# Projections of the next head group one unit earlier, and that group's weight split moved between two output scalings

## The chip, the core and the metric

The kernel runs on one core of one Trainium2 chip. The metric is the device time of one execution in microseconds (us); less is better. The engines are TensorE (PE in the profile; its weight loads are PEld), VectorE (DVE), ScalarE (ACT), GpSimd (POOL) and SyncE (SP), which here only issues DMAs. Each engine works through its own instructions in order and waits on semaphores for the others. SBUF is the on-chip memory, PSUM the banks that TensorE writes.

## What is computed

One hybrid transformer layer over x of 4 batches, 1024 tokens and 512 features, float32. The part that matters here is its first block, causal attention with 16 heads of 32:

```python
kqv = x @ Wqkv + bqkv                      # x: 4 x 1024 x 512
q, k, v = parts of 512 features each       # 16 heads of 32
scores = einsum('bsnh,btnh->bnst', k, q) / sqrt(32)    # upper triangle kept
attn = softmax(scores, axis=2)
out = einsum('bnkq,bnkh->bqnh', attn, v) @ Wo + bo
```

After it come an expert feed-forward block, a state-space block and the feed-forward block once more. The change touches none of them.

## The kernel before

A loop runs over the 4 batches. In the attention part of a batch the 16 heads form 4 groups of 4 (a group is 128 of the 512 features), and a group forms 2 pairs of 2 heads: the first pair has `hf` 0 and the second `hf` 1, so a batch has 8 pairs, p0 to p7, and a new group begins at each even one.

The work of a pair is cut into 12 units, u0 to u11, each a block of 128 keys by up to 512 queries. TensorE issues, in this order by hand: in unit u the scores of unit u+1 (`scores_b`, L859), then the weighing of the values by unit u's exponentials (`weigh`, L876 and L878), then, in u2 to u7, score tiles of the next pair of which only the row maxima are wanted (`scores_a`, L839; 16 tiles, `AHEAD` says which in which unit; a tile waits for a certain number of earlier maxima, as it takes their banks). In u9 the 16 maxima are transposed for the next pair. In the last unit the scores are already those of the next pair's u0.

In the first pair of a group that is not the last, TensorE also makes the next group's projections: four chunks (`project`, L724 to L726), each 12 matmuls of 512 columns into PSUM bank 7, one behind each unit named in `PROJECT_AT`. A chunk's result is read by ScalarE (`project_hi`, L1214, the rounded part, behind the exponential of the unit after) and then by VectorE (`project_lo`, L1541, the remainder); both write `EV`. When the fourth chunk's remainder is there, SyncE copies `EV` by 12 DMAs into the stacks `QS` and `KS` of the next group's first pair (L463), six for each head. `scores_a` in u2 of the second pair reads the first six.

VectorE takes the row maxima (L1565). The outputs and the softmax sums of 512 queries (a half, c 0 or c 1) lie in PSUM bank 6. `take` (L1571) copies them to `OS`, in u3 for half 0 and behind u11 for half 1. `invert` (L1578) makes `rec`, the reciprocals: in two parts in u8 and u9 for half 0, and in one part behind the second `take` for half 1. GpSimd then multiplies `OS` by `rec` (L1870, the output scaling, `o_scaled`). A `take` waits until GpSimd has scaled the half before it, because it writes over `OS`; and the first weighing into bank 6 for a new half (u0 for half 0, u4 for half 1) waits for that `take`. VectorE's order in a pair is this:

```python
for u in range(UNITS):
    if u == 3:
        take(p, 0)
    if not (last and hf):
        for t16 in AHEAD.get(u, ()):
            maximum(p + 1, t16)
    if hf == 0 and not last and u in PROJECT_AT:
        project_lo(g + 1, PROJECT_AT.index(u), False)
    if u in (8, 9):
        invert(p, hf, 0, u - 8, 2)
take(p, 1)
invert(p, hf, 1, 0, 1)
```

The weights of a group arrive by two DMAs in `win_raw`. ScalarE rounds them (`group_hi`, L1184, in u1 of the first pair, `qkw_hi`), GpSimd subtracts the rounded part (`group_lo`, L1808, `qkw_lo`), and the first projection chunk waits for that. Semaphore waits are written `signal.wait(engine, n, k)`, which means that k events of round n have happened. GpSimd also copies a group's values to `VG` (L1833).

Of the kernel before, what the change touches and what calls it, by code (L numbers as in the profile page):

```python
# [29 lines left out]
GROUPS = HEADS * HS // P  # L30
# [9 lines left out]

AHEAD = {2: (0, 1, 2, 3), 3: (4, 5), 4: (6, 7), 5: (8, 9, 10, 11), 6: (12, 13), 7: (14, 15)}
TURN_AT = 9
PROJECT_AT = (4, 6, 8, 10)

MAX_BANK = [0, 1, 2, 3, 0, 2, 0, 2]
MAX_FREE = [-1, -1, 0, 0, 2, 4, 5, 6]
# [90 lines left out]
def hybrid_layer(nc, x, Wqkv, bqkv, Wo, bo, W_in, conv_w, conv_b, z_bias, Dskip, W_out,  # L137
                 Wr, br, Wd, bd, Wu, bu, out):
    with ExitStack() as ctx:
# [6 lines left out]
        def signal(name, per):  # L146
            return Signal(sem(name), per)
# [101 lines left out]
        qkw_lo = signal("qkw_lo", 1)  # L249
# [441 lines left out]
        def _(pe):  # L691
# [100 lines left out]
            with pe.Fori(0, NB) as b:  # L792
# [20 lines left out]
                def project(g, ch, first=False):  # L813

                    w, c = ch // 2, ch % 2
                    if ch == 0:
                        qkw_lo.wait(pe, b * 4 + g, 1)
                    elif not first:
                        pj_lo.wait(pe, b * 4 + g, ch)
                    cols = slice(c * HB, (c + 1) * HB)  # L820
                    for k in range(KT):
                        i = three(ps[:, 4 + ch if first else 7, :], win[:, 0, w, 0, k, :], win[:, 0, w, 1, k, :],
                                  uh[:, k, cols], ul[:, k, cols], k == 0, k == KT - 1)
                    i.then_inc(pj.sem, 1)

                def scores_a(p, slot, occ, t16):

                    hh, t = t16 // TT, t16 % TT
                    if t == 0:
                        pe.wait_ge(s_stack[slot][hh], occ * 96 + 96)  # L830
                    free = MAX_FREE[t] + hh * TT
                    if free > 0:
                        a_max.wait(pe, p, free)
                    b0 = MAX_BANK[t]
                    n = (t + 1) * P
                    for c in range(0, n, HB):
                        m = min(HB, n - c)
                        diag = c + m == n
                        i = pe.matmul(ps[:, b0 + c // HB, 0:m], QS[slot][0:STACK, hh, t * P:(t + 1) * P],  # L839
                                      KS[slot][0:STACK, hh, c:c + m], start=True, stop=not diag)  # L840
                        if diag:
                            i = pe.matmul(ps[:, b0 + c // HB, m - P:m], identb[:, :], mask_ts[:, :], start=False, stop=True)  # L842
                    i.then_inc(a_pe.sem, 1)
# [71 lines left out]
                for last in (False, True):  # L915
                    with (pe.Fori(0, GROUPS - 1) if not last else ExitStack()) as i_:
                        g = GROUPS - 1 if last else i_
                        for hf in range(2):
# [3 lines left out]
                            for u in range(UNITS):  # L922
# [9 lines left out]
                                if ahead:  # L932
                                    for t16 in AHEAD.get(u, ()):
                                        if t16 == 2:
                                            ex.wait(pe, p, 3)
                                        scores_a(p + 1, 1 - hf, occ + hf, t16)
                                if hf == 0 and not last and u in PROJECT_AT:
                                    project(g + 1, PROJECT_AT.index(u))

# [193 lines left out]
        def _(act):  # L1133
# [27 lines left out]
            def experts(n, f, meanwhile=None):  # L1161
                def exponentials(h):
                    hs = slice(h * HALF, (h + 1) * HALF)
                    g_in.wait(act, f, h + 1)
                    act.activation(gex[:, hs, :], ge_[:, hs, :], ACT.Exp).then_inc(g_exp.sem, 1)

                turn(n, range(HALF + 2))
                exponentials(0)
                turn(n, range(HALF + 2, TT))
                if meanwhile is not None:  # L1170
                    meanwhile()
                for t in range(TT):
                    if t == 1:

                        exponentials(1)
                    t_pe.wait(act, f, t + 1)
                    if t >= 2:
                        u_pe.wait(act, f, t - 1)
                    act.copy(hgT[:, t % 2, :], ps[:, t % 2, 0:P])
                    act.copy(w3T[:, t % 2, :], ps[0:3 * E, t % 2, P:2 * P]).then_inc(t_act.sem, 1)  # L1180

            def group_hi(n):
                act.wait_ge(s_qkw, n * 32 + 32)
                act.copy(win[:, 0, :, 0], win_raw[:, 0, :, 1]).then_inc(qkw_hi.sem, 1)  # L1184
# [18 lines left out]
            with act.Fori(0, NB) as b:  # L1203

                def project_hi(g, ch, first):
                    w, c = ch // 2, ch % 2
                    if ch == 0 and not first:

                        for i in range(2):
                            for hh in range(2):  # L1210
                                act.wait_ge(s_stack[i][hh], (b * 4 + g) * 96)
                    pj.wait(act, b * 4 + g, first_at(ch) if first else ch + 1)
                    act.sem_inc(s_tick, 1)
                    act.activation(EV[w][0][:, c * HB:(c + 1) * HB], ps[:, 4 + ch if first else 7, :], ACT.Identity,  # L1214
                                   bias=bqk[:, w * GROUPS:w * GROUPS + 1] if first else
                                   bqk[:, bass.ds(g + w * GROUPS, 1)]).then_inc(pj_hi.sem, 1)
# [17 lines left out]
                for last in (False, True):  # L1234
                    with (act.Fori(0, GROUPS - 1) if not last else ExitStack()) as i_:
                        g = GROUPS - 1 if last else i_
                        for hf in range(2):
                            p = b * 8 + g * 2 + hf
                            for u in range(UNITS):
# [5 lines left out]
                                if hf == 0 and not last and u == 1:  # L1245
                                    group_hi(b * 4 + g + 1)
                                if hf == 0 and not last and u - 1 in PROJECT_AT:
                                    project_hi(g + 1, PROJECT_AT.index(u - 1), False)
                experts(b * 4 + 1, b * 2)
# [107 lines left out]
        def _(dve):  # L1357
# [170 lines left out]
            with dve.Fori(0, NB) as b:  # L1528
# [32 lines left out]
                def maximum(p, t16):  # L1561
                    hh, t = t16 // TT, t16 % TT
                    a_pe.wait(dve, p, t16 + 1)
                    b0 = MAX_BANK[t]
                    dve.tensor_reduce(mneg[:, hh, t:t + 1], wide(b0)[:, 0:(t + 1) * P], AX.X, ALU.max, negate=True).then_inc(a_max.sem, 1)  # L1565
# [21 lines left out]
                for last in (False, True):  # L1587
                    with (dve.Fori(0, GROUPS - 1) if not last else ExitStack()) as i_:
                        g = GROUPS - 1 if last else i_
                        for hf in range(2):  # L1590
                            p = b * 8 + g * 2 + hf
# [9 lines that stand above are left out]
# [144 lines left out]
        def _(pool):  # L1745
# [49 lines left out]
            def until(sig, n, k):  # L1795
                sig.wait(pool, n, k)
                pool.sem_inc(s_tick, 1)
# [8 lines left out]
            def lo_in_place(hi, lo, raw):  # L1806

                return pool.tensor_tensor(lo, raw, hi.bitcast(F32), ALU.subtract)  # L1808

            def group_lo(n):  # L1810
                until(qkw_hi, n, 1)
                lo_in_place(win[:, 0, :, 0], win[:, 0, :, 1], win_raw[:, 0, :, 1]).then_inc(qkw_lo.sem, 1)
# [10 lines left out]
            with pool.Fori(0, NB) as b:  # L1823
# [21 lines left out]
                def residual():  # L1845

                    for t in range(TT):
                        pool.wait_ge(s_out[t], b * 16 + 16)
                        pool.sem_inc(s_tick, 1)
                        i = pool.tensor_tensor(X[:, t, :], XN[:, t, :], bob[:, :], ALU.add)  # L1850
                    i.then_inc(s_bias, 1)
                    pool.wait_ge(s_bias, b + 1)
                    pool.sem_inc(s_tick, 1)

                for which in range(3):
                    first, last = which == 0, which == 2
                    with (pool.Fori(1, GROUPS - 1) if which == 1 else ExitStack()) as i_:
                        g = 0 if first else GROUPS - 1 if last else i_
                        for hf in range(2):
                            p = b * 8 + g * 2 + hf  # L1860
                            if hf == 0 and not last:
                                group_lo(b * 4 + g + 1)
                                until(qkw_lo, b * 4 + g + 1, 1)
                                if first:
                                    residual()
                            for c in range(2):
                                until(o_rec, p, c + 1)
                                dst = OT[hf * 64:(hf + 1) * 64, g, c * HB:(c + 1) * HB] if isinstance(g, int) else \
                                    OT[hf * 64:(hf + 1) * 64, bass.ds(g, 1), c * HB:(c + 1) * HB].rearrange("p a t -> p (a t)")
                                pool.tensor_tensor(dst, OS[hf * 64:(hf + 1) * 64, :], rec[hf * 64:(hf + 1) * 64, :], ALU.mult).then_inc(o_scaled.sem, 1)  # L1870

                                until(o_scaled, p, c + 1)
                            if not last:
                                values(g + 1, hf)
                                until(vg_done, p + 2, 1)
# [91 lines left out]
```

## Time and profile before

| | us |
|---|---|
| median of 3 runs | 3203.94 |
| the 3 runs | 3199.12, 3222.03, 3203.94 |
| the profiled execution, its time | 3217.47 |
| its span, first to last instruction | 3215.6 |
| TensorE busy in it | 3021.2 (94%) |
| VectorE busy | 2083.9 (65%) |
| ScalarE busy | 1119.2 (35%) |
| GpSimd busy | 751.5 (23%) |
| mean granted TensorE clock | 0.963 |

The time of an execution is its span and about 2 us around it. The profiled execution is 13.5 us above the median of the three. The attention pairs of the four batches lie at 138 to 373, 910 to 1159, 1695 to 1943 and 2480 to 2728 us of the span. Rows of the timeline are in order of time; the busy share of TensorE counts modelled ends, so waits are read from the idle time in brackets behind an instruction.

### The profile page before, as it was taken

How to read it: one execution, taken by the hardware profiler on the slowest of the kernel's cores; microseconds unless marked ns; L12 is line 12 of the kernel's file. 1: busy time of each engine (PE TensorE's matmuls, PEld its weight loads, DVE VectorE, ACT ScalarE, POOL GpSimd, SP SyncE). 2: the span in 40 equal slices, each digit the busy share in tenths (PEclk: the TensorE clock that was granted, in tenths of full speed). 3: DMA queues.
4: the chain of work that ended last, by engine and by line, in shares of the span. 5: the costliest groups of instructions: out<-in, count | busy, mean ns of one | idle time of the engine just before them, and what ended most of it. 6: DMA issues, size and time to landing. Idle time of an engine off the chain costs nothing.

```text
span 3215.6 us, 59395 instructions
## 1 busy us (share of the span) xinstructions
PE 3021.2 (94%) x20772; PEld 2060.6 (64%) x20772; DVE 2083.9 (65%) x2942; ACT 1119.2 (35%) x1749; POOL 751.5 (23%) x1061
## 2 busy tenths in 40 slices
PE   3899999999999999999989999999998999999998
PEld 3654477777654447777764544877775554677776
DVE  2566565777756665677675666477775666647777
ACT  2133234444123323444322332444421333244442
POOL 3211112334121101333302110133322111023332
PEclk7999999999989999999998999999999999999999
DMA  9322111111232202111132220211123222021112
GB/s 337 83 54 58 28 52 49 50 45 50 73 66 46 66 21 53 46 51 46 38 93 53 66 46 14 66 43 51 38 67 87 46 46 47 14 75 44 52 45 76
DMA packets 163746, 191.55 MB, mean 60 GB/s; under 512 B 43962, under 2 KB 103994, under 8 KB 161786
## 3 DMA queue, kind: packets, MB, share of 16 engines
q1 hardware_dynamic: 157150, 175.83, 20.2%
q10 hardware_dynamic: 6432, 13.63, 1.4%
q8 instruction: 90, 1.47, 0.2%
q14 instruction: 74, 0.61, 0.1%
HBM read 106.99 MB, written 23.36 MB: 41 GB/s over the span
## 4 chain that ended last, share of the span: by engine, by line
PE 77%; DVE 9%; issue 4%; SPq 4%; DMA 4%; ACT 1%; POOL 1%; ACTq 0%; DVEq 0%; POOLq 0%
PE ps L724 14%; PE ps L725 13%; PE ps L726 13%; PE ps L876 8%; PE ps L839 6%; PE ps L859 5%; PE ps L1059 4%; PE ps L943 3%; PE ps L1045 2%; PE ps L1105 2%; PE ps L1068 2%; DMA KS<-EV 2%; DVE mneg L1565 1%; PE ps L734 1%; PE ps L842 1%
## 5 line engine op out<-in xcount | busy, mean ns | idle before, releaser
L724 PE MATMUL ps<-uh,win 128*128 128x512 f32 x1536 | 626.9, 408 | 11.2 <-POOL win L1808 10.5
L725 PE MATMUL ps<-ul,win 128*128 128x512 f32 x1536 | 600.9, 391 | 0.0
L726 PE MATMUL ps<-uh,win 128*128 128x512 f32 x1536 | 600.5, 391 | 0.0
L1565 DVE TENSOR_REDUCE mneg<-ps 128x1 f32<-128x128 f32 (+7 forms) x512 | 363.3, 752 | 168.1 <-PE ps L842 162.7
L1242 ACT ACTIVATE PR<-ps 128x1024 f32<-128x1024 f32 (+3 forms) x384 | 310.1, 809 | 434.8 <-PE ps L862 293.2
L876 PE MATMUL ps<-PR,VG 128*32 128x512 f32 (+3 forms) x1536 | 350.2, 533 | 12.3 <-DVE OS L1571 8.2
L724 PEld LDWEIGHTS ps<-uh,win 128*128 128x128 f32 x1536 | 288.6, 188 | 104.9 <-issue 29.6
L878 PE MATMUL ps<-PR,ones 128*32 128x512 f32 (+3 forms) x1536 | 350.1, 533 | 0.0
L726 PEld LDWEIGHTS ps<-uh,win 128*128 128x128 f32 x1536 | 288.3, 188 | 64.8
L1677 DVE TENSOR_TENSOR LM<-ps,LM 128x512 f32<-128x512 f32 x256 | 170.1, 685 | 242.3 <-PE ps L1059 198.5
L1908 POOL TENSOR_SCALAR_AFFINE_SELECT LM<-LM 128x512 f32<-128x512 f32 x256 | 208.7, 826 | 491.9 <-ACT LM L1318 491.9
L725 PEld LDWEIGHTS ps<-ul,win 128*128 128x128 f32 x1536 | 289.1, 188 | 53.1
L859 PE MATMUL ps<-QS,KS 97*128 97x512 f32 (+3 forms) x768 | 272.2, 421 | 10.0 <-ACT PR L1242 6.6
L839 PE MATMUL ps<-KS,QS 96*128 96x512 f32 (+3 forms) x768 | 250.5, 425 | 28.8 <-DMA KS<-EV 21.1
L1870 POOL TENSOR_TENSOR OT<-OS,rec 64x512 f32<-64x512 f32 (+1 forms) x64 | 82.4, 1287 | 812.6 <-DVE rec L1578 812.6
L1665 DVE SCALAR_TENSOR_TENSOR Ct<-ps,cpt,Ct 128x1023 f32<-128x1023 f32 (+2 forms) x192 | 245.5, 1279 | 14.4 <-ACT Ct L1308 9.8
L1665 DVE SCALAR_TENSOR_TENSOR Bt<-ps,cpt,Bt 128x1023 f32<-128x1023 f32 (+2 forms) x192 | 243.4, 1267 | 1.8 <-ACT Bt L1308 1.6
L839 PEld LDWEIGHTS ps<-KS,QS 96*128 96x128 f32 x768 | 142.9, 214 | 144.1 <-DVE mneg L1565 58.9
L859 PEld LDWEIGHTS ps<-QS,KS 97*128 97x128 f32 x768 | 146.6, 205 | 132.8 <-issue 85.9
L1158 ACT CAST uh<-ps 128x512 fp32r<-128x512 f32 x128 | 73.6, 587 | 419.1 <-PE ps L734 419.1
L1578 DVE RECIPROCAL rec<-OS 64x256 f32<-64x256 f32 (+1 forms) x96 | 214.6, 2261 | 2.1
L1318 ACT ACTIVATE LM<-ps 128x512 f32<-128x512 f32 x256 | 147.5, 601 | 124.6 <-PE ps L1045 124.6
(219 smaller groups left out, 5007.3 us busy)
## 6 DMA issues: line engine op xcount, KB each, us to landing
raw<-in_t SPq DMA_DIRECT2D x128, 256.0 KB, 2.8
QS<-EV SPq DMA_DIRECT2D x192, 128.0 KB, 2.5
KS<-EV SPq DMA_DIRECT2D x168, 128.0 KB, 2.6
in_t<-tiles ACTq DMA_DIRECT2D x10, 1024.0 KB, 8.5
XN<-in_L_attn_a_x_dram SPq DMA_DIRECT2D x40, 256.0 KB, 5.0
win_raw<-in_L_attn_a_Wqkv_dram SPq DMA_DIRECT2D x34, 256.0 KB, 3.4
win_raw<-in_t SPq DMA_DIRECT2D x32, 256.0 KB, 2.7
edec<-ed_t SPq DMA_DIRECT2D x512, 16.0 KB, 1.6
```

The source lines that it names most:

```text
L724: pe.matmul(dst, hi_l, hi_r, start=first, stop=False)
L725: pe.matmul(dst, hi_l, lo_r, start=False, stop=False)
L726: return pe.matmul(dst, lo_l, hi_r, start=False, stop=last)
L839: i = pe.matmul(ps[:, b0 + c // HB, 0:m], QS[slot][0:STACK, hh, t * P:(t + 1) * P], KS[slot][0:STACK, hh, c:c + m], start=True, stop=not diag)
L859: i = pe.matmul(ps[:, SCORE_BANK[u] + hh, 0:n], KS[slot][:, hh, s * P:(s + 1) * P], QS[slot][:, hh, t0:t0 + n], start=True, stop=not diag)
L876: pe.matmul(ps[o:o + HS, 6, at:at + n], VG[:, s, h:h + HS], PR[:, u % 2, hh, 0:n], start=(s == 0), stop=last)
L878: i = pe.matmul(ps[r:r + HS, 6, at:at + n], ones[:, 0:HS], PR[:, u % 2, hh, 0:n], start=(s == 0), stop=last)
L1242: act.activation(PR[:, u % 2, :, 0:n], ps[:, SCORE_BANK[u]:SCORE_BANK[u] + 2, 0:n], ACT.Exp, scale=SCALE).then_inc(ex.sem, 1)
L1565: dve.tensor_reduce(mneg[:, hh, t:t + 1], wide(b0)[:, 0:(t + 1) * P], AX.X, ALU.max, negate=True).then_inc(a_max.sem, 1)
L1578: i = dve.reciprocal(rec[hf * 64:(hf + 1) * 64, cols], OS[(1 - hf) * 64:(2 - hf) * 64, cols])
L1665: dve.scalar_tensor_tensor(dst[:, par, k:L], wide(2 * w)[:, 0:L - k], cpt[:, par, w, at:at + 1], dst[:, par, k:L], ALU.mult, ALU.add).then ...
L1908: pool.affine_select(out=v, in_=v, compare_op=ALU.is_ge, fill=0.0, base=0, pattern=[[0, 4], [1, P]], channel_multiplier=-1).then_inc(sel_p ...
```

## The change

`PROJECT_AT` goes from (4, 6, 8, 10) to (3, 5, 7, 9). TensorE, ScalarE and VectorE all take the places of the chunks from it. GpSimd's order changes too: the split of group 1's weights stays at the start of the batch's pairs, ahead of the residual; that of groups 2 and 3 moves from behind the second scaling and the copy to `VG` of the group before (p1 and p3) to between the two output scalings of p1 and p3. GpSimd's wait for ScalarE's `group_hi` of those weights, which happens in u1 of the pair behind, moves with it.

```diff
-PROJECT_AT = (4, 6, 8, 10)
+PROJECT_AT = (3, 5, 7, 9)
...
+                group_lo(b * 4 + 1)
+                until(qkw_lo, b * 4 + 1, 1)
+                residual()
                 for which in range(3):
-                    first, last = which == 0, which == 2
-                    with (pool.Fori(1, GROUPS - 1) if which == 1 else ExitStack()) as i_:
-                        g = 0 if first else GROUPS - 1 if last else i_
+                    two_more, last = which == 0, which == 2
+                    with (pool.Fori(0, GROUPS - 2) if two_more else ExitStack()) as i_:
+                        g = i_ if two_more else GROUPS - 3 + which
                         for hf in range(2):
                             p = b * 8 + g * 2 + hf
-                            if hf == 0 and not last:
-                                group_lo(b * 4 + g + 1)
-                                until(qkw_lo, b * 4 + g + 1, 1)
-                                if first:
-                                    residual()
                             for c in range(2):
+                                if two_more and hf and c:
+                                    group_lo(b * 4 + g + 2)
+                                    until(qkw_lo, b * 4 + g + 2, 1)
                                 until(o_rec, p, c + 1)
```

## Rows read from the trace of the kernel before

**Rows 1.** The page: TensorE's busy time with the others, and its granted clock by slice.

```profile
PE 3021.2 (94%) x20772; PEld 2060.6 (64%) x20772; DVE 2083.9 (65%) x2942; ACT 1119.2 (35%) x1749; POOL 751.5 (23%) x1061
...
PEclk7999999999989999999998999999999999999999
```

**Rows 2.** TensorE's waits, whole run: us in total, times, longest us.

```profile
PE ps L839 <- DMA KS<-EV: 21.1, 17, 1.4
...
PE ps L724 <- POOL win L1808: 10.5, 10, 2.0
...
PE ps L876 <- DVE OS L1571: 8.2, 28, 0.3
```

**Rows 3.** Windows, one pair each: length, busy times, granted clock, DMA share, GB/s.

```profile
236.24:262.68 26.44, 24.23 (x181) 11.18 (x183) 19.98 (x22) 9.97 (x14) 2.73 (x4) 1.00 0.32 73
...
952.02:983.04 31.02, 28.84 (x181) 13.25 (x181) 20.39 (x22) 9.96 (x15) 2.71 (x4) 0.83 0.28 63
1018.50:1048.03 29.53, 27.31 (x181) 12.35 (x181) 20.17 (x22) 9.96 (x14) 2.72 (x4) 0.88 0.29 65
...
327.41:352.38 24.97, 24.18 (x181) 11.19 (x184) 19.22 (x21) 9.97 (x14) 3.27 (x4) 1.00 0.33 79
```

**Rows 4.** Windows inside p3 of the second batch, same columns.

```profile
1023.40:1026.80 3.40, 1.98 (x17) 1.11 (x11) 1.50 (x5) 0.51 (x1) 1.86 (x2) 1.00 0.93 201
1026.80:1033.60 6.80, 6.80 (x30) 2.86 (x30) 2.89 (x4) 1.41 (x2) 0.00 (x0) 0.50 0.21 46
```

**Rows 5.** Timeline of TensorE in p2, p3 and p6 of the first batch.

```profile
209.45 0.30 PE L859 MATMUL ps<-QS,KS 97*128 97x128 f32 x1
...
230.85 0.73 PE L859 MATMUL ps<-QS,KS 97*128 97x512 f32 x2
...
232.51 0.50 PE L724 MATMUL ps<-uh,win 128*128 128x512 f32 x1
...
235.36 0.40 PE L859 MATMUL ps<-QS,KS 97*128 97x512 f32 x1
...
238.00 0.62 PE L876 MATMUL ps<-PR,VG 128*32 128x512 f32 x1 [0.30 <-DVE OS L1571]
...
242.79 0.33 PE L839 MATMUL ps<-KS,QS 96*128 96x128 f32 x1 [1.42 <-DMA KS<-EV]
...
340.50 0.44 PE L839 MATMUL ps<-KS,QS 96*128 96x384 f32 x1 [0.29 <-DVE mneg L1565]
```

**Rows 6.** Timeline of VectorE around the two pair boundaries of p2, first batch.

```profile
202.67 3.35 DVE L1578 RECIPROCAL rec<-OS 64x512 f32<-64x512 f32 x1
...
208.77 0.69 DVE L1571 COPY OS<-ps 128x512 f32<-128x512 f32 x1 [0.60 <-PE ps L878]
...
231.47 3.36 DVE L1578 RECIPROCAL rec<-OS 64x256 f32<-64x256 f32 x2
236.38 0.75 DVE L1541 SCALAR_TENSOR_TENSOR EV<-ps,bqk,EV 128x512 fp32r<-128x512 f32 x1 [1.54 <-ACT EV L1214]
237.26 0.69 DVE L1571 COPY OS<-ps 128x512 f32<-128x512 f32 x1
237.98 3.35 DVE L1578 RECIPROCAL rec<-OS 64x512 f32<-64x512 f32 x1
```

**Rows 7.** Timeline of GpSimd in the same stretch.

```profile
208.70 2.37 POOL L1808 TENSOR_TENSOR win<-win_raw,win 128x1024 fp32r<-128x1024 f32 x1 [0.43 <-POOL VG L1833]
235.11 1.31 POOL L1870 TENSOR_TENSOR OT<-OS,rec 64x512 f32 x1 [24.03 <-DVE rec L1578]
```

**Rows 8.** Timeline of ScalarE there, and in p4 of the second batch.

```profile
202.71 1.04 ACT L1184 CAST win<-win_raw 128x1024 fp32r<-128x1024 f32 x1
...
235.66 0.69 ACT L1214 ACTIVATE EV<-ps,bqk 128x512 fp32r<-128x512 f32 x1 [3.02 <-PE ps L726]
...
1051.31 1.05 ACT L1184 CAST win<-win_raw 128x1024 fp32r<-128x1024 f32 x1 [1.38 <-DMA win_raw<-in_L_attn_a_Wqkv_dram]
```

**Rows 9.** Timeline of the DMA queue of SyncE, behind p2.

```profile
237.25 1.77 SPq L463 DMA_DIRECT2D QS<-EV  x3
```

## The prediction

> **What bounds the kernel now.** I read the page first. TensorE is busy for 94% of the span, and its clock dips only slightly [rows 1]. So only two things can move the time: waits of TensorE, and stretches in which its clock is low. Its waits come next. The three that the change can touch are 21.1 us for the `KS` stack, 10.5 us for a weight split by GpSimd (a row that state-space waits share) and 8.2 us for the copy `OS` [rows 2]. Then I cut the attention part into windows, one per pair. A second pair of a group without a fall of the clock (p3 of the first batch) takes 26.44 us, and p6, which has the same work and no late stack, takes 24.97 [rows 3]. The 1.47 between them is the wait of 1.42 at the first `scores_a` [rows 5]. All 12 second pairs that follow projections have it, in four batches.
>
> Ten of these 12 are longer still, because their clock falls. Six of them are like p3 of the second batch (29.53 us at a mean clock of 0.88), one (p5 of the first batch) is 29.39, and three are like p1 of the second (31.02 at 0.83) [rows 3]. The fall comes right behind the wait: the stretch with the wait in it is at 1.00, and the next 6.8 us are at 0.50, which is 1.2 GHz [rows 4]. Against 26.44 that is about 3.1 us seven times and 4.6 us three times, 35 us in all. So the late stack costs 12 x 1.42 = 17 us directly and 35 through the clock, and these 52 us are what could be gained.
>
> **The fourth chunk one unit earlier.** I follow p2 of the first batch. The chunk takes 232.51 to 235.36, 2.85 us. It now goes ahead of the scores of u11 and the weighing of u10, so it starts at 230.85 and ends at 233.70 [rows 5]. ScalarE follows 0.30 behind (235.66), VectorE's remainder 0.72 behind that and takes 0.75 [rows 6, 8]. The remainder is done at 235.47 instead of 237.13, and the stack's DMAs, 0.12 behind it [rows 9], start 1.66 earlier. Their first half would be there at 242.79 - 1.66 = 241.13, before TensorE could use it (242.79 - 1.42 = 241.37). So the wait for `KS` goes.
>
> What is late next is on VectorE. In its loop `project_lo` of a unit stands ahead of `invert` of that unit. Before, both parts of `invert` ran together in the gap of u8 and u9 (231.47, 3.36 for both [rows 6]) and the fourth remainder came after them. Now the fourth remainder belongs to u9 and stands ahead of the second part, and it can't begin before 234.72. Queued behind it are the second part, 235.47 to 237.15; GpSimd's scaling of half 0, which starts 0.28 after the reciprocals and takes 1.31 [rows 6, 7], so 237.43 to 238.74; and then `take` of half 1, which writes over `OS`. Before, `take` started at 237.26, as soon as the last weighing was done. Now it starts at 238.74 plus the hand-over from GpSimd to VectorE. No row has that hand-over into a `take`, since no `take` waited for GpSimd. Its bounds are 0.05 (`take` to weighing: 237.95 to 238.00) and 0.28 (reciprocal to GpSimd); I use 0.1, nearer the plain hand-over, as GpSimd's longer one holds register work of its own. `take` is then 238.84 to 239.53, and the first weighing of p3 is at 239.58 instead of 238.00, 1.58 later. The wait there grows from 0.30 [rows 5] to 1.88. The first `scores_a` comes at 241.37 + 1.58 = 242.95 instead of 242.79. **Net: +0.16 per group, 12 x 0.16 = +1.9 us** (1.3 to 4.1 for the bounds). One wait has taken the place of the other.
>
> The following steps hold this shift. The long reciprocal of half 1 ends at 239.56 + 3.35 = 242.9 and is off VectorE before the first maximum. Its scaling ends near 244.5, and `take` in u3 comes 6.1 us behind the start of that reciprocal, as in p2 (202.67 to 208.77 [rows 6]), so near 245.7, and there is no second wait.
>
> **The other three chunks.** They are the same matmuls, so TensorE's work is the same. The second and third only trade places with a unit's scores and weighing; their readers on ScalarE and VectorE need 0.30 + 0.69 and 0.75 us and fall into the 2.85 us and more that VectorE idles there. The first, though, leaves its place behind the score tiles 6 and 7, the long ones. In p6, where nothing stands there, the third tile of u5 waits 0.29 us for a maximum [rows 5]. In the first pairs that wait was covered by the chunk and now isn't. It costs 0.29 in a pair at full clock; in p0 of three batches the clock is low there, so nine times: **+2.6 us** (0 to 3.5).
>
> **The split between the scalings.** In p1 and p3 GpSimd now waits for ScalarE's rounding in u1 of the next pair, with the scaling of half 1, the copy to `VG` and, through `o_scaled`, `take` in u3 behind it. In p2 the rounding is done at 203.75 [rows 8]; the split takes 2.37 [rows 7], so about 203.9 to 206.3. The reciprocal it would have waited for anyway ends at 206.02 [rows 6]. The scaling so starts at about 206.6 and ends at 207.9, and `take` in u3 is at 208.77 [rows 6]: 0.9 us of slack. The first chunk is due at 209.45, where the scores of u5 start now [rows 5], 3 us behind the split. In the old order (208.70 + 2.37 = 211.07) it would have waited 1.6 us, so this part pays for the earlier first chunk and gives nothing more. The chunk is also a cover: it stands between the maxima tiles and the weighing that needs `take`, so `take` may be over 2 us late at no cost. In p4 of the second batch the weights landed late, and ScalarE began 1.38 us later than it could have [rows 8]; the scaling then ends at 209.3 on p2's times and `take` is 0.5 us late, under that cover. **0 us.**
>
> VectorE's reciprocal runs beside the split for the first time; no row shows such a pair. If the two exclude each other, the split starts at 206.02 and ends at 208.4, the scaling at 209.9, `take` comes 1.2 us late, and the cover still holds. The Trainium skill ("SBUF — State Buffer", Who interferes with whom) says that GpSimd shares a port pair with VectorE, but that an instruction with one SBUF input outside the two-port modes does not contend; by it the price is 0, and no row here shows it.
>
> **The clock.** A fall followed a wait of 1.42 us in 10 of 12 cases and not in the other two, in pairs with the same work. So where a wait lies against the chip's own time decides too. The new wait, 1.88 in one piece at the start of the pair, is longer than the old 1.42, so I expect falls at least as often. The profiled execution with its 10 falls is 13.5 us above the median of the runs; if falls make that difference, the median run has some 22 us of them, six or seven. The Trainium skill ("TensorE: Matmul & The Clock Gate", What's actually happening) says that the gate watches on a clock of its own that doesn't restart with the kernel; this case's trace agrees, as two of 12 like waits had no fall.
>
> **The sum.** Against the profiled execution: 3217.5 + 1.9 + 2.6 = 3222. Against the median, with as many falls as there: 3204 + 4.5 = 3208.5, and one fall more or less is 3.1.
>
> **Rivals.**
> 1. The falls become rarer, since the new wait is followed by dense work and not by maxima. For: two waits without a fall. Against: the wait is longer. With none at all: 3208 - 22 = 3186. Chance 0.12.
> 2. The `take` isn't held up (my order of VectorE is wrong, or the scaling is ready earlier than I think), so both the wait and its falls go, and the second pairs become like p6. 3204 - 17 - 22 + 2.6 = 3168. For: p6 itself. Against: the order in the loop, which leaves VectorE idle until 234.72. Chance 0.07.
> 3. On the slow side: the longer wait brings a fall every time, and of the long kind (4.6), as in p1. It decides when the wait is long enough to be seen wherever it lies: 12 x 4.6 = 55 instead of 22, so 3208 + 33 = 3241. For: three falls of 10.2 us behind 1.42. Against: these three came in one pair, p1, behind a p0 that had itself run at the low clock. Chance 0.11.
> 4. GpSimd in front of the first chunk: the weights land over 3 us later than `group_hi` needs them, in all 8 places, and TensorE waits for the split: with 1.5 us each, 3208 + 12 = 3220. In the trace they were late once in 8, by 1.5 us. Chance 0.04.
>
> The forecast has 0.66. The range reaches from rival 1 to short of rival 3: 3182 to 3232. A measurement of this kernel can tell about 1%, 32 us, from no change: faster than 3172 only rival 2 and an edge, 0.07; slower than 3236 rival 3, 0.10; within, 0.83.
>
> **What would show it.** In the profile after: no wait of `scores_a` for `KS`; the wait of the weighing for `OS` up from 0.3 to about 1.9 in 12 places, some 27 us in all, with `take` released by GpSimd; the second part of `invert` apart from the first and behind the fourth remainder; 12 waits of 0.3 for a maximum in first pairs, or nine; the split done before the scaling of half 1 in p1 and p3 and no wait of a projection for it in attention. Wrong would be: `take` still released by TensorE; second pairs of 25 us; or falls in a number other than 6 to 12.

## The result and the profile after

The changed kernel is slower. Its median is 3251.01 us over 10 runs (3236.31 to 3262.09), against 3213.69 us over 10 runs of the kernel before. The ratio is 1.0103, with a 95% interval of 1.0074 to 1.0133, or 33 us. (The ratios, here and below, leave out runs more than 1.5% above the fastest of the same kernel; the medians keep them.) The forecast of 3208.5 was wrong, and the time lies outside its range. The profiled execution took 3236.88 us, at the low end of its runs.

TensorE's waits over the whole run, in the changed kernel (us in total, times, longest us), and behind them VectorE's wait for GpSimd:

```profile
PE ps L876 <- DVE OS L1571: 27.5, 28, 2.0
PE ps L724 <- POOL win L1808: 11.6, 8, 2.0
PE ps L839 <- DVE mneg L1565: 10.7, 30, 0.8
...
PE ps L839 <- DMA KS<-EV: 5.8, 7, 1.2
```

```profile
DVE OS L1571 <- POOL OT L1871: 20.2, 13, 1.7
```

Against [rows 2] the wait for `KS` has gone from 21.1 to 5.8 us and that for `OS` has come from 8.2 to 27.5, with `take` now released by GpSimd. One wait has replaced the other, as forecast. VectorE around p2 and p3 of the first batch, to be held against [rows 6]:

```profile
230.31 1.75 DVE L1578 RECIPROCAL rec<-OS 64x256 f32<-64x256 f32 x1
235.43 0.75 DVE L1541 SCALAR_TENSOR_TENSOR EV<-ps,bqk,EV 128x512 fp32r<-128x512 f32 x1 [3.37 <-ACT EV L1214]
236.21 1.75 DVE L1578 RECIPROCAL rec<-OS 64x256 f32<-64x256 f32 x1
239.58 0.69 DVE L1571 COPY OS<-ps 128x512 f32<-128x512 f32 x1 [1.61 <-POOL OT L1871]
```

The two parts of the reciprocals are torn apart. VectorE idles for 3.37 us behind the first, waiting for ScalarE's part of the fourth chunk, and the second comes only behind the remainder. GpSimd and TensorE in the same stretch, against [rows 5, 7], with VectorE's long reciprocal ahead of them:

```profile
202.86 3.35 DVE L1578 RECIPROCAL rec<-OS 64x512 f32<-64x512 f32 x1
204.12 2.37 POOL L1808 TENSOR_TENSOR win<-win_raw,win 128x1024 fp32r<-128x1024 f32 x1 [2.43 <-ACT win L1184]
206.91 1.30 POOL L1871 TENSOR_TENSOR OT<-OS,rec 64x512 f32 x1 [0.41 <-POOL win L1808]
...
238.22 1.25 POOL L1871 TENSOR_TENSOR OT<-OS,rec 64x512 f32 x1 [29.16 <-DVE rec L1578]
```

```profile
217.04 0.45 PE L839 MATMUL ps<-KS,QS 96*128 96x384 f32 x1 [0.30 <-DVE mneg L1565]
...
231.52 0.50 PE L724 MATMUL ps<-uh,win 128*128 128x512 f32 x1
...
240.32 0.62 PE L876 MATMUL ps<-PR,VG 128*32 128x512 f32 x1 [1.91 <-DVE OS L1571]
```

The wait of the first weighing is 1.91 us (forecast 1.88), and the third tile of u5 waits 0.30 (forecast 0.29). The split (204.12 to 206.49) overlaps VectorE's reciprocal (202.86 to 206.21) for 2.09 us and takes 2.37 us, exactly as before, so the two don't exclude each other. The Trainium skill ("SBUF — State Buffer", Who interferes with whom) says that a VectorE instruction with one SBUF input, outside the two-port modes, doesn't contend with GpSimd; this trace agrees.

What the forecast did not price is what comes behind these waits. These are windows of the changed kernel with the columns of [rows 3]: p1, p2 and p3 of the first batch, then the wait in p3 and the stretch behind it.

```profile
174.47:201.11 26.64, 24.19 (x181) 11.20 (x184) 20.26 (x22) 9.97 (x13) 3.90 (x4) 1.00 0.32 73
201.11:236.94 35.83, 35.21 (x229) 20.09 (x232) 21.36 (x25) 13.18 (x19) 4.86 (x4) 1.00 0.23 49
236.94:269.58 32.64, 30.24 (x181) 13.79 (x183) 20.67 (x22) 9.97 (x14) 3.86 (x4) 0.79 0.26 59
238.00:241.40 3.40, 1.49 (x13) 0.52 (x13) 1.79 (x2) 0.38 (x1) 1.25 (x1) 1.00 0.90 196
241.40:255.10 13.70, 13.70 (x62) 6.61 (x62) 6.68 (x8) 2.81 (x4) 1.90 (x2) 0.50 0.26 57
```

A second pair without a fall takes 26.64 us, 0.2 more than the 26.44 of [rows 3], as forecast. Behind the 1.9 us wait in p3, though, the clock is at 0.50 (1.2 GHz) for 13.7 us, against 6.8 in [rows 4], and the pair takes 32.64 instead of 29.53. One second pair of the third batch, p5, had 30.7 us at the low clock and took 39.43:

```profile
1875.48:1914.91 39.43, 37.59 (x181) 16.99 (x184) 21.24 (x22) 9.97 (x13) 4.47 (x4) 0.61 0.20 44
1879.80:1910.50 30.70, 30.70 (x136) 14.79 (x132) 16.46 (x19) 6.27 (x8) 1.91 (x2) 0.50 0.12 26
```

### The profile page after: what moved, and what is told of

The parts are those of the page before. It is cut to its first block, busy times and chain, and to the rows that moved or that the text cites. A ratio compares the mean times of both kernels' runs of the same rounds, so it can differ in the third digit from the quotient of the medians.

```text
span 3235.1 us, 59387 instructions
## 1 busy us (share of the span) xinstructions
PE 3031.6 (94%) x20772; PEld 2071.8 (64%) x20772; DVE 2087.7 (65%) x2942; ACT 1118.4 (35%) x1749; POOL 751.7 (23%) x1061
## 4 chain that ended last, share of the span: by engine, by line
PE 76%; DVE 10%; issue 5%; SPq 3%; DMA 3%; ACT 2%; POOL 1%; ACTq 0%; DVEq 0%; POOLq 0%
PE ps L724 14%; PE ps L725 13%; PE ps L726 13%; PE ps L876 7%; PE ps L839 5%; PE ps L859 5%; PE ps L1059 4%; PE ps L943 3%; PE ps L1045 2%; DVE mneg L1565 2%; PE ps L1105 2%; PE ps L1068 2%; PE ps L734 1%; DVE stats L1369 1%; PE ps L1078 1%
## 5 line engine op out<-in xcount | busy, mean ns | idle before, releaser
L876 PE MATMUL ps<-PR,VG 128*32 128x512 f32 (+3 forms) x1536 | 346.3, 528 | 32.2 <-DVE OS L1571 27.5
L1871 POOL TENSOR_TENSOR OT<-OS,rec 64x512 f32 (+1 forms) x64 | 82.3, 1286 | 802.4 <-DVE rec L1578 799.1
L839 PE MATMUL ps<-KS,QS 96*128 96x512 f32 (+3 forms) x768 | 248.2, 420 | 16.5 <-DVE mneg L1565 10.7
```

The source lines that it names most:

```text
L876: pe.matmul(ps[o:o + HS, 6, at:at + n], VG[:, s, h:h + HS], PR[:, u % 2, hh, 0:n], start=(s == 0), stop=last)
```

## The experiments

Ten experiments ran, one of them (`changed_again`) with the changed kernel itself. The table gives the length of TensorE's wait at the start of the second pair, or in u2 where marked; the median and its runs; the ratio to the kernel before with its interval; the time at the low clock, 2 x (1 - mean clock) x time, as a mean over the runs; and time x mean clock, which is what the execution would take if low stretches counted half. The last two are worked out from each run's time and granted clock. The experiments ran in three sets, each with runs of the kernel before beside it, whose medians were 3221.8 (29 runs, beside `recip_first`, `pool_only`, `pool_old_order` and `last_chunk_back`), 3218.7 (14) and 3217.5 (17). Over the 29 runs the kernel before has 237 us at the low clock (230 over those that the ratios count) and a time x clock of 3103.

| kernel | wait | median us (runs) | ratio, 95% interval | low-clock us | time x clock |
|---|---|---|---|---|---|
| changed | 1.9 | 3251.0 (10) | 1.0103 (1.0074 to 1.0133) | 286 | 3107 |
| changed_again | 1.9 | 3243.9 (7) | 1.0100 (1.0068 to 1.0132) | 276 | 3108 |
| pool_only | 1.4 in u2 | 3219.2 (10) | 1.0003 (0.9969 to 1.0038) | 241 | 3103 |
| last_chunk_back | 1.4 in u2 | 3230.9 (12) | 1.0025 (0.9999 to 1.005) | 252 | 3107 |
| pool_old_order | 1.9 | 3236.4 (10) | 1.0060 (1.0022 to 1.0097) | 242 | 3118 |
| recip_first | 0.3 | 3170.1 (6) | 0.9821 (0.9786 to 0.9856) | 142 | 3098 |
| wait_11_at_start | 1.2 | 3178.2 (4) | 0.9873 (0.9835 to 0.9911) | 145 | 3106 |
| wait_14_at_start | 1.5 | 3193.1 (12) | 0.9943 (0.9908 to 0.9979) | 181 | 3105 |
| wait_19_at_start | 1.9 | 3250.6 (6) | 1.0106 (1.0072 to 1.014) | 291 | 3103 |
| stack_06_later | 2.1 in u2 | 3243.1 (6) | 1.0093 (1.0057 to 1.0129) | 283 | 3106 |
| units_4_6_7_9 | 0.3 | 3170.6 (6) | 0.9876 (0.9815 to 0.9936) | 170 | 3086 |

**The reciprocals first.** The first experiment undoes only the order on VectorE that the moved chunk made.

```diff
-                                if hf == 0 and not last and u in PROJECT_AT:
-                                    project_lo(g + 1, PROJECT_AT.index(u), False)
-                                if u in (8, 9):
-                                    invert(p, hf, 0, u - 8, 2)
+                                if u == 9:
+                                    invert(p, hf, 0, 1, 2)
+                                if hf == 0 and not last and u in PROJECT_AT:
+                                    project_lo(g + 1, PROJECT_AT.index(u), False)
+                                if u == 8:
+                                    invert(p, hf, 0, 0, 2)
```

> The changed kernel with one more edit: in u9 of a first pair VectorE makes the second part of the reciprocals ahead of the fourth remainder, not behind it. Theory W (the cost is the wait that the fourth remainder puts in front of the copy to OS, with the falls of the clock behind it): the copy is due at the last weighing again, the wait for OS is 0.3 us, the KS wait stays away, all 12 second pairs take 25.0 us without a fall, first pairs some 35.7. Against the kernel before that is 12 x 1.5 = 18 us less, 35 us less of falls and 4 us more in the first pairs: ratio 0.983 to 0.987. Rival P (the kernel is slower because its rows stand differently against the chip's clock gate, so that falls come wherever there is a short wait, and because the first pairs are longer): the falls stay, ratio 0.995 to 1.01. Rival C (the chunks one unit earlier cost by themselves, through maxima and PSUM bank 7): first pairs over 36.5 us and ratio over 1.00.

It measured 0.9821, 2.8% below the changed kernel's ratio and just under the range written for theory W. A window over p1, then VectorE behind p2 of the first batch:

```profile
178.68:203.66 24.98, 24.19 (x181) 11.19 (x183) 19.23 (x21) 9.99 (x14) 2.62 (x3) 1.00 0.35 77
```

```profile
233.42 3.36 DVE L1578 RECIPROCAL rec<-OS 64x256 f32<-64x256 f32 x2
238.52 0.75 DVE L1541 SCALAR_TENSOR_TENSOR EV<-ps,bqk,EV 128x512 fp32r<-128x512 f32 x1 [1.74 <-ACT EV L1214]
241.05 0.69 DVE L1571 COPY OS<-ps 128x512 f32<-128x512 f32 x1 [1.78 <-PE ps L878]
```

Both parts run together ahead of the fourth remainder, and `take` is released by TensorE again. All 12 second pairs take 24.95 to 24.98 us and none has a fall. Together they take 299.6 us against 352.5 before: 52.9 us, where the prediction had read 52 us to be gained (17 of waits, 35 through the clock). The early fourth chunk is worth that; the changed kernel throws it away by one order of two instructions. Theory W stands; P and C fall.

**GpSimd's order alone, and the chunks alone.** Two kernels separate the two parts of the change: GpSimd's new order with `PROJECT_AT = (4, 6, 8, 10)`, and the kernel before with `PROJECT_AT = (3, 5, 7, 9)`.

> GpSimd's new order alone, the projections in units 4, 6, 8 and 10 as before. Theories W and C: the split ends some 5 us earlier, nobody wants it earlier, ratio 0.998 to 1.003, split rows of 2.37 us, the copy in u3 of p2 and p4 not later than before. Rival G (GpSimd's split beside VectorE's reciprocal, or its wait for the weights, holds the copy in u3 up): second-half copies released by GpSimd in p2 and p4 and ratio 1.003 to 1.01.

> The projections in units 3, 5, 7 and 9, GpSimd's order as before. By the prediction's step the first chunk of p2 and p4 waits 1.6 us for the split (8 times, 13 us) on top of what the changed kernel has, so ratio 1.012 to 1.018 against before; p0's chunk doesn't wait. If the cover of that chunk were worth nothing, the ratio would be the changed kernel's, 1.010.

The first measured 1.0003, with an interval of 11 us either way: GpSimd's part costs and brings nothing that shows by itself. In the second, the first chunk of p2 waits for the split in the old place (GpSimd, then TensorE, first batch):

```profile
225.53 2.36 POOL L1808 TENSOR_TENSOR win<-win_raw,win 128x1024 fp32r<-128x1024 f32 x1 [0.43 <-POOL VG L1833]
```

```profile
227.94 0.59 PE L724 MATMUL ps<-uh,win 128*128 128x512 f32 x1 [1.47 <-POOL win L1808]
```

Time x clock is 11 us above the changed kernel's, near the 13 forecast for eight such waits. But the ratio, 1.006, missed its expectation (1.012 to 1.018): this kernel had 242 us at the low clock, 44 less than the changed kernel. The intervals of the two overlap, and why its clock fell less was not found.

**The fourth chunk back in u10.** `PROJECT_AT = (3, 5, 7, 10)`, all else as changed.

> The changed kernel with the fourth chunk back in u10 (units 3, 5, 7, 10). Theory W: the fourth remainder comes behind both reciprocals again, OS waits are 0.3 us and the KS wait of 1.4 us is back, second pairs 26.4 without and 29.5 with a fall, first pairs 0.3 to 0.4 longer than before: ratio 1.000 to 1.003. Rival C (the first three chunks are what costs): ratio 1.007 to 1.012 as in the changed kernel.

It measured 1.0025. A first pair (p2) and a second pair (p1) of the second batch:

```profile
990.43:1026.25 35.82, 35.20 (x229) 20.02 (x232) 21.48 (x24) 13.26 (x19) 6.16 (x5) 1.00 0.23 49
963.99:990.43 26.44, 24.23 (x181) 11.18 (x182) 19.98 (x22) 9.96 (x15) 2.57 (x3) 1.00 0.33 73
```

So the first three chunks cost 0.4 us in a first pair and 3 to 4 us in all by time x clock, and the second pairs are those of before. By the ratios 8 of the 33 us are left, with an interval of 0 to 16, so some 25 hang on the fourth.

**The wait by itself, in four lengths.** The kernel with the reciprocals first got one more, idle, VectorE instruction, which holds `take` up. It leaves the computation as it is.

```diff
+                            if hf == 0 and not last:
+                                dve.reciprocal(rec[64:128, 0:512], bvb[64:128, 0:512])
                             take(p, 1)
```

> The kernel with the reciprocals first, plus one idle VectorE instruction ahead of the second copy to OS in first pairs that have projections: a reciprocal of 64x512 of a constant into a part of rec that nobody reads. It ends 3.35 us behind the fourth remainder and so holds the copy up by some 1.6 us, as the changed kernel does, with GpSimd, the remainder and the stack out of it. Theory W (the 1.9 us wait at the start of the second pair is the whole cause): OS waits of 1.9 us, ratio to before 1.007 to 1.013, time x clock 3105 to 3109. Rival S (the cause is in how GpSimd's scaling, SyncE's stack and the copy follow each other): ratio under 1.003.

> The same with 400 columns: the wait for OS is 1.1 us. Directly that is 12 x 0.85 = 10 us over the kernel with the reciprocals first. If falls of the clock need a wait about as long as the old one (1.42): no falls in second pairs, 25.8 us each, ratio 0.984 to 0.989. If any wait over a few tenths brings falls in proportion: ratio 0.994 or more.

> The reciprocals first, and the idle VectorE instruction with 438 columns: the wait for OS is some 1.4 us, as long as the KS wait of the kernel before. Second pairs without a fall 26.1 us. If the cost through the clock grows in proportion to the wait from 1.1 on: halfway between the kernels with 1.1 and 1.9, ratio 0.996 to 1.001. If it comes all at once above 1.4: no falls, ratio 0.988 to 0.991. The kernel before has a 1.42 wait at another place and falls in 10 of 12; if that is the rule here too, the ratio is 0.998 to 1.003.

With 512 columns the changed kernel's time is back (1.0106), although VectorE has the reciprocals first and `take` no longer waits for GpSimd, whose order is still the changed kernel's. Rival S is out. Time x clock, 3103, is a little under what was written for it. The 13.7 us falls are back too, six of them; these are a whole pair and the fall in it, in p3 of the second batch:

```profile
1030.50:1062.83 32.33, 30.22 (x181) 13.74 (x184) 22.35 (x22) 9.97 (x14) 2.62 (x3) 0.79 0.27 60
1035.60:1049.30 13.70, 13.70 (x61) 6.39 (x61) 6.69 (x9) 2.81 (x4) 1.92 (x2) 0.50 0.22 47
```

With 400 columns the wait is 1.2 and not one of the 12 second pairs has a fall. With 438 it is 1.5 and three have one. These are p3 of the second batch with 400, then p5 and p3 of the first batch with 438:

```profile
1012.20:1038.08 25.88, 24.17 (x181) 11.19 (x184) 21.15 (x22) 9.98 (x13) 2.62 (x3) 1.00 0.33 74
```

```profile
299.27:331.30 32.03, 30.22 (x181) 13.84 (x184) 21.83 (x22) 10.00 (x14) 2.67 (x3) 0.79 0.25 54
237.24:263.37 26.13, 24.18 (x181) 11.20 (x184) 21.41 (x22) 10.00 (x13) 2.61 (x3) 1.00 0.33 74
```

Each step of the wait costs 12 times its length directly: 11 us for the first (12 x 0.91), 3 for the second (12 x 0.26), 5 for the third (12 x 0.44). The medians rise by 8, 15 and 57 us; by the ratios, which allow for the sets, it is 17, 23 and 52. The time at the low clock goes from 142 us to 145, 181 and 291. So up to 1.2 us a wait brought no more of it; from 1.5 to 1.9 it cost some ten times its added length, and the difference is the clock. The 1.5 us kernel lay between the values I had written for all-or-nothing and for proportion.

**A longer wait at the old place.** In the kernel before, one DMA of the second head's stack was put ahead of the last one of the first head's.

```diff
+            if hf == 0 and len(which) == 2:
+                jobs = jobs[:5] + [jobs[6]] + [jobs[5]] + jobs[7:]
```

> The kernel before with one DMA of the second head's stack put ahead of the last one of the first head's, in the stack of a group's first pair: the wait for KS in u2 grows from 1.42 to about 2.0 us, as long as the changed kernel's 1.9 but at its old place, 12 x 0.6 = 7 us directly. If the length of the wait makes the longer falls: ratio 1.009 to 1.014, falls of 13.7 us in second pairs. If the place does (the start of the pair against u2): ratio 1.002 to 1.004, falls of 6.8 and 10.2 us as before.

It measured 1.0093, the value written for the length. Its waits, and p3 of the first batch with the fall in it:

```profile
PE ps L841 <- DMA KS<-EV: 30.1, 18, 2.1
```

```profile
249.90:277.20 27.30, 27.30 (x111) 12.29 (x113) 15.62 (x18) 5.82 (x8) 0.00 (x0) 0.50 0.06 14
241.87:280.38 38.51, 36.16 (x181) 16.00 (x182) 20.82 (x22) 9.97 (x15) 3.31 (x4) 0.65 0.24 57
```

About 0.6 us more in u2 takes the ratio from 1 to 1.009, and three of its falls last 27.3 us, not the 13.7 that I had expected. In the median the place hardly matters at 2 us; in the profile it does, as 11 of the 12 second pairs have a fall, against seven and six in the changed kernel's two. At 1.4 to 1.5 the place matters more: 3 of 12 falls at the start of the pair, 10 of 12 in u2, where a wait of 0.3 stands a few us ahead.

**The changed kernel again, and a version of both.** The first is for times beside the doses. The second takes the kernel before, puts the reciprocals first and has `PROJECT_AT = (4, 6, 7, 9)`, with GpSimd's order untouched.

> The changed kernel as it is, for a second profile and for times beside the next three. Its ratio to before 1.010; time x mean clock some 3107 us against 3103 before; the wait for OS 1.9 us in 12 places, some of them followed by stretches of about 14 us at the low clock.

> The kernel before, GpSimd's order as it was, with the chunks in units 4, 6, 7 and 9 and the reciprocals ahead of the fourth remainder. The first chunk keeps its place behind the long score tiles, so first pairs should be 35.3 to 35.4 us instead of 35.7, and second pairs 25.0 with no fall. Ratio 0.979 to 0.983 if the first two chunks' move and GpSimd's new order bring nothing; 0.985 or more if the earlier first chunk or split matter after all.

The changed kernel came out at 1.0100, as before. In its second profile six second pairs had a fall, five of 13.7 us and one of 17.1. The other has first pairs of 35.24 us and second pairs of 24.99 (p2 and p3 of the third batch):

```profile
1749.28:1784.52 35.24, 34.94 (x229) 19.98 (x232) 22.15 (x25) 13.30 (x18) 6.09 (x5) 1.00 0.23 50
1784.52:1809.51 24.99, 24.20 (x181) 11.21 (x185) 19.24 (x21) 9.98 (x13) 2.61 (x3) 1.00 0.33 77
```

Its median, 3170.6, is that of `recip_first`, 3170.1. Its ratio, 0.9876, missed the 0.979 to 0.983 that I had written for the case that the rest brings nothing, and lies in the other range (0.985 or more); but its interval (0.9815 to 0.9936) holds both, and its second pairs are as short. So it is not shown whether the earlier first chunks or GpSimd's new order bring anything beside the reciprocals first and the early fourth chunk; by the median they don't.

Its time x clock, 3086, is 12 us below that of `recip_first`, and its low-clock time 28 us above, more than its shorter first pairs explain. Part of it is that the product takes too much off. These are p0 of the first batch in it and in `recip_first`:

```profile
139.68:179.21 39.53, 39.53 (x217) 21.92 (x221) 18.53 (x23) 12.04 (x18) 14.59 (x11) 0.83 0.19 41
143.66:178.68 35.02, 33.72 (x217) 19.59 (x221) 18.19 (x23) 11.94 (x18) 14.69 (x11) 1.00 0.21 46
```

With 13.7 us at the low clock the pair takes 4.5 us more, where half of 13.7 would be 6.8: the 1.30 us in which TensorE is idle in the second window are gone in the first. The product takes off the half all the same. The rest of the 12 us is not explained. Both kernels beat the kernel before and the changed one, the first by 1.8% and 2.8%.

## Why the prediction was wrong

The path and its sizes held up to the new wait. The `KS` wait of the second pairs went and the `OS` wait came, 1.91 us for 1.88. Second pairs without a fall grew by 0.2 for 0.16, first pairs mostly by 0.3 to 0.5 for 0.29. The wait for a maximum came in the three low-clock p0 too, which the prediction had left out: 10.7 us in 30 waits, for this before:

```profile
PE ps L839 <- DVE mneg L1565: 7.4, 19, 0.8
```

That is 3.3 us, for the term of 2.6. The one term that no row had, the hand-over from GpSimd to `take`, was put at 0.1 and measured 0.11 (238.22 + 1.25 to 239.58). GpSimd's part cost nothing and its split didn't slow down. Time x clock, in which the clock hardly counts, rose by 4 us, for a forecast of 4.5.

The step that failed is "The clock", and with it "The sum". It said that the longer wait would bring falls "at least as often" and then entered them "with as many falls as there", at no price. The runs put that price at most of the result: 286 us at the low clock for 230 to 237, and 276 for 229 in the second set. At half speed that is 24 to 28 of some 33 us. I had counted falls, and should have asked how long one lasts. In the profile there are seven in second pairs, fewer than the 10 of before. But five are 13.7 us long, one 30.7 and one 3.4, where before they were 6.8 or 10.2; one of 13.7 costs 6.0 us (32.64 against 26.64), where one of before cost 3.1 or 4.6. Rival 3 had the right mechanism, a longer wait that brings a longer kind of fall. It put 33 us on the clock, where the runs show 24 to 28, by a wrong count (all 12) and too short a fall (10.2 us, 4.6 in cost), so that its total, 37 above its base, is near the measured 33 partly by luck; it had 0.11.

The evidence for it was in the trace. Waits of 1.42 us had falls behind them that cost 3.1 or 4.6 us, so a wait cost up to four times its length in all; that is a steep place to lengthen a wait by a third. From the two of 12 without a fall the prediction concluded that the place of a wait in time decides too. The profiles agree (see the last section), but it doesn't follow that the cost of the falls stays.

The base was off as well. The median of three runs was 3204, that of the later 10 was 3213.7 and those beside the experiments were 3217 to 3222. Against 3213.7 the same sum is 3218, still 33 us short. The "six or seven" falls of the median run, 22 us, came from that same median of three: over 29 runs the kernel before has 237 us at the low clock in the mean, and its profiled execution, with 10 falls, has 242.

Rival 2 named the time of a kernel in which `take` isn't held up, 3168. The kernel with the reciprocals first is that kernel, at 3170. That the two times agree is partly luck: the rival lies 36 us below its base of 3204, and the kernel measured 52 below the 3221.8 beside it, as base and falls were both put too low.

What stays open is where the added low-clock time lies. In the two profiles of the changed kernel the second pairs have 102 and 85 us of it against 79 before, and take 363.2 and 354.9 us together against 352.7. Over all runs it rose by 49 us, and by 48 in the second set. In the first profile about half of the 19 us over the profile of before lies outside the attention pairs. Both profiled executions are among the two fastest of their runs, with 255 and 238 us at the low clock for means of 286 and 276, so they show less of it than a typical run. That the wait causes the loss is shown by the kernels that differ in it alone; that all of the loss lies in the falls right behind it isn't.

## What to carry to other kernels

When a step is moved earlier on the engine that makes it, look at every engine that reads it: on an in-order engine it moves ahead of other work there too, and the work behind it then waits for the producer. A wait of the matmul engine must be priced with the clock behind it, and by its length in one piece. Compare time x mean clock beside time; it showed an effect of 4 us in runs that spread over 30, but it is no clean separation, as the 3086 of `units_4_6_7_9` shows.

## What the runs showed of the hardware

The response to the length of a wait was steeper than expected. With the same wait 12 times in an execution, 1.2 us brought no fall, 1.5 us three in 12, and 1.9 us six or seven, most of them of 13.7 us. The medians were 3178, 3193 and 3251 us. Once fallen, the clock stayed at 1.2 GHz for 13.7, 27.3, 30.7 and, in p1 of the first batch of `pool_old_order`, 34.1 us, although TensorE was busy throughout:

```profile
180.42:214.55 34.13, 34.13 (x147) 15.51 (x143) 19.19 (x20) 7.22 (x10) 1.90 (x2) 0.50 0.13 28
```

Which of the like waits has a fall behind it is not spread evenly. In the three profiles with a wait of 1.9 us (the changed kernel twice and `wait_19_at_start`) all 12 p3 fell, for 13.7 us each, but only two of the 12 p1 and six of the 12 p5, in pairs with the same work. In `pool_old_order`, with the same wait and p2 and p4 some 1.5 us longer or more, it was one of four p3, three of four p1 and three of four p5. This fits the prediction's view that the place of a wait in time matters; no run moved a wait in time and nothing else. Runs of one kernel differ by 20 to 40 us, and nearly all of it goes with the clock: over the runs of the kernel before, 3184 us goes with a mean clock of 0.975 and 3232 us with 0.959.
